# Graph attention kernel on one Trainium2 core: the weighted values of a tile are summed in instructions of 512 columns, and VectorE adds the four partial sums

## The reference

```
q = (x @ Wq + bq), k = (x @ Wk + bk), v = (x @ Wv + bv)      # [n, 4, 32] each
attn = einsum('nhc,mhc->hnm', q, k) / sqrt(32)
alpha = softmax of attn over the neighbours m with adj[n, m] != 0   (0 for a row without any)
out = einsum('hnm,mhc->hnc', alpha, v)                       # transposed to [n, C*H]
x_r = x @ Ws + bs
beta = sigmoid(concat([out, x_r, out - x_r]) @ Wb)
y = x + beta * x_r + (1 - beta) * out
result = (y - mean(y)) / sqrt(var(y) + 1e-5)
```

## Time and profile before

| | |
|---|---|
| median of 3 runs | 2172.78 us |
| execution that was profiled | 2167.49 us (span 2165.6 us) |
| PE matmul busy | 1175.3 us (54%), 4636 records |
| PE weight load busy | 707.2 us (33%), 4696 records |
| DVE busy | 1315.7 us (61%), 3427 records |
| ACT busy | 841.0 us (39%) |
| POOL busy | 1119.0 us (52%) |
| chain of waits: another core or an unknown queue | 14% of the span |
| L982, the sum of the slots on PE | 350.4 us busy, 2032 records |

### The profile page before, as it was taken

How to read it: one execution, slowest core, us unless ns; L and a number is a source line. 1 busy time by engine, 2 the same in 40 slices (tenths; PEclk the granted TensorE clock), 3 DMA queues, 4 the chain that set the end, 5 groups by cost and what they waited for, 6 DMA issues and landing times.

```text
span 2165.6 us, 20121 instructions
## 1 busy us (share of the span) xinstructions
PE 1175.3 (54%) x4636; PEld 707.2 (33%) x4696; DVE 1315.7 (61%) x3427; ACT 841.0 (39%) x1595; POOL 1119.0 (52%) x1711
## 2 busy tenths in 40 slices
PE   6303545746646564556457665666477655551454
PEld 5101323424324332334324333343243332240233
DVE  5548776855856485356655565367466745781466
ACT  2304342324633254244443454355456733330112
POOL 4542656455266556665455447545655354557261
PEclk9556666657677576676676777677677766565566
DMA  8826955647576566475476566567677655324120
GB/s 316 337 61 240 268 175 193 237 164 267 192 244 225 190 229 236 167 255 211 158 287 219 208 235 249 198 233 279 212 267 284 221 213 209 97 63 106 54 83 22
DMA packets 130037, 438.70 MB, mean 203 GB/s; under 512 B 26567, under 2 KB 61198, under 8 KB 97150
## 3 DMA queue, kind: packets, MB, share of 16 engines
q1 hardware_dynamic: 76510, 297.15, 37.3%
q0 software_dynamic: 52832, 136.07, 20.5%
q10 hardware_dynamic: 576, 4.19, 0.5%
HBM read 417.93 MB, written 19.44 MB: 202 GB/s over the span
## 4 chain that ended last, share of the span: by engine, by line
DVE 32%; issue 22%; another core or an unknown queue 14%; DVEq 12%; PE 10%; ACT 7%; DMA 1%; ACTq 1%; POOL 0%; SPq 0%; POOLq 0%
DVE s_raw L1229 5%; DVEq L1277 4%; DVE s_kv L1227 4%; DVE s_wtop L1276 4%; ACT s_mask L1004 3%; PE s_ps_w L810 3%; DVE s_kv L1253 2%; PE s_acc L982 2%; DVE s_top L1324 2%; DVEq L1430 2%; DVE s_d_max L1441 1%; DVEq L1331 1%; ACT s_diag L1021 1%; DVE s_wtop L1270 1%
## 5 line engine op out<-in xcount | busy, mean ns | idle before, releaser
L781 POOL DMA_INDIRECT s_kv<-kv_rows,s_rec_in x1023 | 971.8, 950 | 825.1 <-PE s_acc L982 340.3
L810 PE MATMUL s_ps_w<-s_mask,s_bit_w 128*128 128x512 bf16 x1003 | 370.8, 517 | 306.1 <-ACT s_mask L1004 170.0
L1004 ACT ACTIVATE s_mask<-s_adj_in 128x2048 bf16<-128x2048 f32 x252 | 478.4, 1900 | 148.8 <-remote 61.0
L982 PE MATMUL s_acc<-s_kv,ident 128*128 128x128 f32 x2032 | 350.4, 341 | 240.7 <-issue 159.6
L982 PEld LDWEIGHTS s_acc<-s_kv,ident 128*128 128x128 f32 x2032 | 334.7, 255 | 266.0 <-issue 167.7
L810 PEld LDWEIGHTS s_ps_w<-s_mask,s_bit_w 128*128 128x128 bf16 x1008 | 109.1, 119 | 517.9 <-issue 263.5
L1229 DVE TENSOR_REDUCE s_raw<-s_kv 128x48 f32<-128x1536 f32 (+15 forms) x76 | 147.1, 1935 | 12.2 <-issue 6.8
L1253 DVE TENSOR_TENSOR s_kv<-s_kv,s_ps_q 128x1536 f32<-128x1536 f32 (+15 forms) x76 | 146.8, 1931 | 8.8 <-ACT s_ps_q L1043 4.0
L1441 DVE TENSOR_REDUCE s_d_max<-s_ps_key 128x1 f32<-128x1024 f32 x32 | 39.2, 1225 | 185.5 <-remote 159.0
L1227 DVE TENSOR_TENSOR s_kv<-s_kv,s_ps_q 128x1536 f32<-128x1536 f32 (+15 forms) x76 | 147.1, 1936 | 4.4 <-ACT s_or L1035 2.2
L1276 DVE MAX8 s_wtop<-s_words 128x8 f32<-128x512 f32 x171 | 118.8, 695 | 33.4 <-issue 20.7
(11 more groups left out here) (282 smaller groups left out, 1578.8 us busy)
## 6 DMA issues: line engine op xcount, KB each, us to landing
s_adj_in<-in_adj SPq DMA_DIRECT2D x248, 1024.0 KB
s_kv<-kv_rows,s_rec_in POOLq DMA_INDIRECT x1023
kv_rows<-s_kv SPq DMA_DIRECT2D x16, 512.0 KB, 7.2
s_rec_in<-node_records SPq DMA_DIRECT2D x55, 106.0 KB
s_kv<-in_x_cols SPq DMA_DIRECT2D x4, 1024.0 KB, 8.8
s_adj_in<-in_adj ACTq DMA_DIRECT2D x4, 1024.0 KB
s_d_in<-in_x_cols SPq DMA_DIRECT2D x8, 512.0 KB
s_d_v<-kv_rows SPq DMA_DIRECT2D x8, 512.0 KB
```

What stands on the lines that cost most here:

```text
L781: nc.gpsimd.indirect_dma_start(out=kv[0:n, START[k] + s], out_offset=None, in_=kv_dram[:, :], in_offset=bass.IndirectOffsetOnAxis(ap=rec_i ...
L810: last = nc.tensor.matmul(w[:], bit_w[:, slab], mask[:, k % 2, s * WORD:(s + 1) * WORD], start=False, stop=(slab == SLABS - 1))
L982: last = nc.tensor.matmul(acc[:, c * D:(c + 1) * D], ident[:], kv[:, START[k] + s, D:2 * D], start=(s == 0), stop=(s == plain(k) - 1))
L1004: nc.scalar.activation(mask[:, q % 2], adj_in[:, q % ADJ_RING], ACT.Sign, accum_out=edges[:, t, h:h + 1]).then_inc(masked, 1)
```

## The change

PE now adds up to four slots by one instruction. In a tile of one unit the slots stand one behind the other in `kv`, so an instruction can take the values of 4 slots as 512 columns and write them to the four quarters of `acc`: slot 0, 4, 8, ... go to quarter 0, slot 1, 5, ... to quarter 1. `width(p)` is 1 for the nine tiles of several chunks, 4 for tiles with 8 or more plain slots (46 units), 2 for eight late tiles (39, 46, 47, 54, 55, 61, 62, 63). A rest that does not fill the width is added by a narrower instruction ahead of the last. `attend` then has a new instruction on DVE that adds the quarters (or halves) from PSUM into `osum`. By the loops of the two kernels the 1016 products become 543: the units of width 1 keep their 343, 622 slots become 172 instructions, and 51 slots become 28.

```
+def width(p):
+    return 1 if n_chunks(p) > 1 else 4 if SLOTS[p] - FOLDED.get(p, 0) >= 8 else 2
+
+
+def acc_steps(k):
+    m, w = plain(k), width(UNITS[k][0])
+    wide, rest = m // w - 1, m % w
+    at = [(w * i, w) for i in range(wide)]
+    if rest:
+        at.append((w * wide, rest))
+    return at + [(m - w, w)]
...
-                for s in range(plain(k)):
-                    if k in FOLD_UNITS and s == plain(k) - 1:
+                for s, n in acc_steps(k):
+                    ends = s + n == plain(k)
+                    if k in FOLD_UNITS and ends:
                         nc.tensor.matmul(acc[0:FOLD, c * D:(c + 1) * D], fold_w[:], kv[:, START[k] + plain(k), D:2 * D],
                                          start=False, stop=False)
-                    last = nc.tensor.matmul(acc[:, c * D:(c + 1) * D], ident[:], kv[:, START[k] + s, D:2 * D],
-                                            start=(s == 0), stop=(s == plain(k) - 1))
-                    if s in (half(k) - 1, plain(k) - 1):
+                    last = nc.tensor.matmul(acc[:, c * D:(c + n) * D], ident[:], kv[:, START[k] + s:START[k] + s + n, D:2 * D],
+                                            start=(s == 0), stop=ends)
+                    if s <= half(k) - 1 < s + n or ends:
                         last.then_inc(summed, 1)
...
+                else:
+                    nc.vector.tensor_reduce(osum[:], acc[:, 0:width(p) * D].rearrange("p (n c) -> p c n", n=width(p)), AX, ALU.add)
+                    sums = osum[:]
                 nc.vector.tensor_scalar(divisor[:], total, TINY, None, ALU.max)
```

## The result

Four runs of the changed kernel took 2180.65 to 2201.49 us, median 2195.69, beside 2172.55 us of the kernel before (four runs, 2166.74 to 2172.80). The ratio is 1.0103, with a 95% interval of 1.0072 to 1.0135: 1.0% slower, 23 us, where I had forecast 2.0% faster. I call the sessions of the first kind late, since in them TensorE's results are reported late, and the others quiet. The result above is from a late session.

What follows compares the result with a forecast made beforehand. No engine's throughput was taken as the bound; the largest item of the changed part was unexplained waits, 282 us. 2167.49 - 78 + 35 = 2124.5 us, plus 5.3 for the median, gave 2130 us, range 2060 to 2212.

Steps and rivals of the forecast that it cites:

- TensorE, fewer instructions: From 640 us on, 28% fewer TensorE records shrink the chain's 282 us of unexplained waits in proportion, by 78 us.
- TensorE, the wide products: TensorE's sum: same columns in fewer instructions save 3 to 27 us of its time, taken as 0 on the path.
- VectorE, the added reduction: 54 more VectorE instructions ahead of `take_words`, 1.0 us per wide one (bounds 0.61 and 1.02), 49 us in all.
- How much of it is on the path: Of the reduction's 49 us on VectorE, 14 hide in waits for the piece's maximum; 35 us are exposed.
- Code loading: TensorE's instruction fetch, 38 packets: some 7 fewer, saving nothing since fetching is mostly hidden.
- The single records behind a burst: TensorE's queue, depth 64, fills with transposes and sum, then records go singly; the sum would stop filling it.
- The unexplained share: Chain waits from 640 us on whose release no record explains: 282 us, forecast to fall to about 200.
- the second rival: Late TensorE stretches need dense bursts, which one-chunk units stop reaching: perhaps 60% of 282 us go, 2044 us; chance 0.10.
- The first rival: Late TensorE stretches come by time or columns and stay; only VectorE's 29 us are added: 2202 us; chance 0.35.

Runs made afterwards that it cites:

- e17: Changed kernel without VectorE's reduction over the quarters, in a late session: 2175.55 us beside 2171.65 of the kernel before, ratio 1.0005.
- e9: Kernel before, with 511 of 673 sum products in tiles of one unit left out, late session: 2114.58 us beside 2139.34, ratio 0.9907.
- e18: Kernel before, with every second gather of tiles of one unit left out (323 of 1023), late session: 1888.83 us beside 2171.65, ratio 0.8671.
- e10: Kernel before plus 352 gathers of 16 bytes a row into an unread buffer, late session: 2513.49 us beside 2139.34, ratio 1.1787.
- e2: Kernel before plus 54 VectorE reductions whose result nobody reads, quiet session: 1657.11 us, ratio 1.0127.
- e5: The changed kernel itself again, beside the kernel before, in a quiet session: 1656.19 us beside 1637.76, ratio 1.0120.
- e1: Changed kernel without VectorE's reduction over the quarters, quiet session: 1632.25 us beside 1636.56 of the kernel before, ratio 0.9990.
- e13: Kernel before plus 352 gathers of 16 bytes a row into an unread buffer, quiet session: 2039.15 us beside 1636.64, ratio 1.2462.
- e3: Kernel before plus 619 products of 4 columns between slots in tiles of one unit, quiet session: 1739.46 us beside 1636.56, ratio 1.0622.

## Why the prediction was wrong

The step that failed is "TensorE, fewer instructions": the 282 us of unexplained waits would shrink by 28%, 78 us. They did not shrink at all (e17: 327 us and ratio 1.0005 with the reduction taken out; e9: 288 us with three quarters of the sum gone). What they shrink with is GpSimd's gathers (e18: 131 us and 283 us less time). With that term at 0 only the added reduction was left, 22 us on the path.

The one reason I gave for the term could not carry it. I said that the last units, with few TensorE records, had a chain free of such waits. They have few gathers too. GpSimd's gathers in the kernel before by stretch (length, busy, count, clock, DMA share, GB/s):

```profile
640.00:1800.00 1160.00, 548.36 (x578) 0.70 0.64 227
1800.00:2100.00 300.00, 138.19 (x145) 0.60 0.33 100
2100.00:2166.00 66.00, 7.80 (x9) 0.63 0.09 28
```

Nine gathers remain behind 2100 us. Two causes had ended together, and I credited the one that the change touches. I could have counted late reports. Call a semaphore that TensorE raises late when its record comes over 1.5 us after the end of the instruction that raises it. In the trace of the kernel before, of those whose instruction ended while GpSimd issued gathers (two or more from 3 us before to 1 us after), 169 of 342 were late (49%); of those with no gather there, 17 of 192 (9%). TensorE's own density does not explain it: beside gathers 43% were late where it had started 12 or more matmul records in the last 5 us, 61% where it had started fewer. The same count over other traces:

| | gathers beside it | none |
|---|---|---|
| before | 169 of 342 | 17 of 192 |
| e9, three quarters of the sum out | 145 of 313 | 11 of 196 |
| e10, more gathers | 209 of 402 | 5 of 137 |
| e18, half the gathers | 141 of 279 | 7 of 259 |
| e2, quiet session | 0 of 566 | 0 of 115 |

In a late session about half of the reports that fall beside gathers are late, whichever kernel runs; e18 has fewer reports that do. These counts are rough, since the traces of late sessions lack many semaphore records: the one of the kernel before has 9367 of them against 28159 in e2's, which has the same program and one instruction kind more. Most of the missing ones tell of DMAs that landed (2833 of the gathers' against 16323). The page shows that as well: gathers have a time to landing in e5's page (this row) and none in the page before or after.

```profile
s_kv<-kv_rows,s_rec_in POOLq DMA_INDIRECT x1023, 4.1
```

The other steps:

- "TensorE, the wide products": 3 to 27 us of TensorE's time and nothing on the path. Right: in quiet sessions the sum is 320 us busy in e5 against 327 in e2, and without the reduction the ratio is 0.999.
- "VectorE, the added reduction": I took 1.0 us between the bounds 0.61 and 1.02; it is 0.692, and 0.424 for two quarters, in all 35.2 us in place of 49. The prediction's lower value was the nearer one. The Trainium skill (VectorE: DVE Perf Modes, "The perf-mode tier table") has every reduction at one element a cycle, from SBUF as from PSUM; by the estimate that I made of it, some 0.6 us. The row of 0.692 us agrees with it better than the row that I preferred, 1.02 us from SBUF.
- How much of it is on the path: I said 35 of 49, 71%. In quiet sessions 20.8 of 35.2, 59%; in the measured comparison 1.03% of 2172.6 = 22.4 us, 16 to 29 by the interval, 64%. The share was near, in part by luck: I had it hidden where VectorE waits for a piece's maximum, and in quiet sessions 41% is hidden though that wait is 1.9 us in all (e5). The size of the reduction was off.
- Code loading: the packets of instructions went from 38 to 30, where I had estimated 7 fewer.

```profile
q8 instruction: 30, 0.49, 0.1%
```

By the Trainium skill (Runtime: NRT & Kernel Launch, "Instruction fetch mechanics") fetching is mostly hidden, so that this was to save next to nothing; e1 and e17 agree (0.9990 and 1.0005).
- The single records behind a burst became fewer: TensorE's idle time put down to "issue" ahead of the sum fell from 159.6 us in the whole run to 76 in the two rows of L996 above, 58.8 of it in the row of 128 columns, nearly all of which the change leaves as it was. The unexplained share did not fall with it (329 us, where the second rival wanted near 110), so the second rival is refuted too.

The first rival's own sum was 2202 us, 2188 to 2222. It holds 2195.7, with a reduction of 22 us on the path in place of 29. Its reason does not hold as it stands: e9 took columns away and the waits stayed, and half the gathers took more than half of them away.

## What to carry to other kernels

Before a wait of unknown origin is tied to what a change touches, list everything else that rises and falls with it in the same stretches, and count late and punctual cases against each. Test a suspected cause by taking it away: adding more of it may only make its engine the bound, as e13 showed. Here cheaper instructions on an engine that is seldom on the path bought nothing, and the instructions that they cost on the busiest engine were paid at 38% to 64%.

## What the runs showed of the hardware

- One kernel on one chip has two times that are far apart: 1636.6 us in one session and 2171.7 us in a later one of the same chip. Four other sessions, on further chips, showed 1637.8, 1636.6, 1635.8 (quiet) and 2139.3 us. For the changed kernel VectorE's busy time is the same in both kinds (1347.1 us in e5, 1345.8 in the first profile), and TensorE's matmuls have 1052.7 and 1133.1 us at a granted clock of 0.746 and 0.682; most of what is added is idle time before results of TensorE. In the quiet traces 0 to 5 of 700 reports of TensorE are over 1.5 us late. VectorE's longest waits in e5 are for DMAs; these are the first rows:

```profile
DVE s_d_pen L1467 <- DMA s_d_in<-in_adj: 25.4, 4, 7.4
DVE s_kv L1241 <- DMA s_kv<-kv_rows,s_rec_in: 21.0, 3, 12.5
```

- What a late session costs falls when gathers are taken away, all on one chip: kernel before 2171.7 - 1636.6 = 535 us, changed kernel without the reduction 2175.6 - 1632.3 = 543 us, half the gathers of the tiles of one unit 1888.8 - 1597.7 = 291 us. With gathers added it did not rise (474 us against 503, on other chips). Which part of a gather matters (its issue, its descriptors, its bytes or the reports of its landing), by what way it holds up a report of TensorE, and what sets the kind of session, is open: no run could choose its kind. One rival stands untested: the record has a span and a clock for every execution of the experiments, so each was recorded by the profiler, and the late traces are the ones that lack semaphore records. The delay may come with the recording; there is no run without it.
- A reduction over four values that lie 128 apart takes 692 ns from PSUM (46 instructions a run) and 1018 to 1040 ns from SBUF at the same shape (one instruction in each run); over two values 425 ns from both.
- A product of 4 columns (f32, two records, each beside a weight load of 128 columns) added 0.36 us to TensorE's busy time in e3, where one of 128 columns has 0.32 us in e2. Its records are shorter (247 ns against 334), but nothing was saved by having fewer columns.
